# An expert attention's loop, its sections cut anew: next front, own attention, former output in one, and queries and keys loaded in three runs

## The chip, the cores and the metric

The kernel runs on one core of one Trainium2 chip. The metric is the device time of one execution in microseconds, the median of several runs. Besides the runs there is one execution under the hardware profiler, from which all rows come. PE is TensorE, DVE VectorE, ACT ScalarE, POOL GpSimd and SP the queue that issues the direct DMAs.

## The reference

Two transformer layers work on x of 4 x 1024 tokens with 256 channels; every sublayer reads a layer norm of x and is added to it. In the second sublayer of layer 0 each of 4 experts is an attention of its own, with 16 heads of 16 channels, over the tokens whose router picks it:

```python
    for e in range(e_total):
        member = (top2 == e).any(-1)
        ...
        xg = jnp.take_along_axis(x, order[..., None], axis=1)
        ...
        q = (xg @ wq[e] + bq[e]).reshape(b, s, h, hd)
        ...
        att = jnp.einsum('bqhd,bkhd->bhqk', q, k) * sm_scale
        att = jnp.where(validg[:, None, None, :], att, -1000000000.0)
        att = jax.nn.softmax(att, axis=-1)
        y = jnp.einsum('bhqk,bkhd->bqhd', att, v).reshape(b, s, d)
        y = y @ wo[e] + bo[e]
        out = out.at[bidx, order].add(wg[..., None] * y)
```

The first sublayers of both layers are causal attentions over all 1024 tokens of a batch element, the last one is a mixture of 64 expert networks.

## The kernel before

The program has these stages, with a barrier of all engines between them: setup; the first causal attention (`l0`), which also routes tokens and scatters their rows to `xg_d`; the loop over 16 expert units; the second causal attention (`l1`), which gathers the units' outputs from `yg_d`; the expert networks (`last_*`).

A *unit* is one batch element with one expert. Its tokens fill `nt` tiles of 128 rows, 0 to 8; the numbers are known only on the chip, in `cnt`. `unit_loop` (L1496) is a hardware loop in which each engine loads its unit's count and jumps through a tree of choices to a program for that `nt`. Each engine's instructions come from one list of tasks, sorted by nominal times in `unit_order` (L257); every engine walks the list and emits its part (`attention_pe` L381, `attention_act` L530, `attention_dve` L612, `attention_pool` L921, `attention_sp` L998). `Waits` puts a semaphore wait where a task needs another's result.

The tasks of a unit, in the order of its list:

- `mk`, `wo`: SP loads the mask row of the keys and the output weights.
- `xt`: PE transposes the rows in XF (L401), ACT copies them to XT.
- `qp`: four projections, of queries and keys for two halves (`g2`) of the heads (L386). ACT writes the result twice (L567, L568), POOL splits it into three bf16 parts in PH (`spl`, L976 to L980), SP stores PH to `qk_d` (`qs`, L1029) and loads it back into QS or KS with the heads apart and 16 channels on partitions, six blocks of 16 rows (`ql`, L1037).
- `vp`: the values (L417), copied to VA. `bv`, `bb`: the value bias through the output weights (L503).
- `nx` (`next_unit`, L1103): SP loads the next unit's rows into XF and its weights.
- For each of four groups `g` of four heads: `s1`, a first pass of the scores (L430), whose maxima DVE reduces (L627); `mh`, `ml`, `mt`, `mr`: the negated maxima become two rows that SP copies from MR to QS (L1046); then `s2`, the second pass (L448), whose exponentials ACT writes to P (L597), and `pv` (L470), the product with the values. `po` and `nt` turn and normalise the result into ON. The second pass of a group runs beside the first pass of the following one.
- `yt` (L486), `op` (L495, released by DVE L699), `yo` (L1081): transposition, output projection, store to `yg_d`.

The tasks that use the large PSUM tiles share two *slots* in turn; a slot is free again when ACT or DVE has copied or reduced it. At the end SP waits for all its DMAs, then all engines meet in `barrier` (L1477), in which SP clears the semaphores, and jump back. So nothing of one unit runs beside another but the loads of `nx`.

The causal layers use the same tasks, from `causal_order` (L191), with four batch elements running into each other. Their `qs` and `ql` have the forms above with 1024 tokens.

## Time and profile before

| What | Value |
|---|---|
| Median of 3 runs | 5252.07 us (5250.45 to 5259.73) |
| Profiled execution, its own time | 5252.09 us |
| Its span | 5250.3 us |
| PE busy | 3697.0 us, 70% |
| DVE busy | 2276.7 us, 43% |
| ACT busy | 2038.4 us, 39% |
| POOL busy | 1158.3 us, 22% |
| Mean granted TensorE clock | 0.830 |

The span goes from the first to the last instruction. Busy is the time in which an engine had an instruction under way. A clock of 1.0 is 2.4 GHz, 0.5 is 1.2 GHz; a stretch in which both were granted shows a value between. DMA is the mean busy share of 16 DMA engines. In a timeline a row gives start, length, engine, line and operation, and in brackets how long the engine had been idle and what ended that; an fp32 matmul counts as two instructions. The sixteen units stand between 955 and 3592 us, with 6, 2, 3 and 7 tiles, four times over.

### The profile page before, as it was taken

The page shows a single profiled execution, that of the slowest core. Times are in us where ns is not written, and L with a number is a line of the kernel's source. Part 1 is how long each engine was busy: PE and PEld are TensorE (multiplying, and loading weights), DVE is VectorE, ACT ScalarE, POOL GpSimd, SP SyncE. Part 2 cuts the span into 40 slices and gives each one's busy share as a digit, 9 for nine tenths or more (in the row PEclk, how much of TensorE's full clock was granted, in tenths as well). Part 3 has the DMA queues.
Part 4 walks back from the last instruction along what each step waited for, and adds up shares of the span by engine and source line. Part 5 has one row for each costly group of instructions (what it writes and reads, how often), then busy time and mean ns, then how long its engine had stood idle before and what let it go on. Part 6 is the DMA issues. An engine that isn't in the chain of part 4 may idle for free. (4 is left out here: it accounts for less than half of the span.)

```text
span 5250.3 us, 56423 instructions
## 1 busy us (share of the span) xinstructions
PE 3697.0 (70%) x20420; PEld 1654.9 (32%) x20421; DVE 2276.7 (43%) x5427; ACT 2038.4 (39%) x4287; POOL 1158.3 (22%) x969
## 2 busy tenths in 40 slices
PE   3888886575696856968569684694488788816765
PEld 1343443232222322223222232222133333304553
DVE  2656663332363423624136251371566666511222
ACT  1555554252272522726226361262254444500111
POOL 2132233100101011010110101102323463471343
PEclk7999998696797967979679796797699899957887
DMA  4745451503404034040340403402524343002456
GB/s 107 151 124 125 98 147 41 96 16 74 85 1 81 12 79 85 1 81 8 82 84 3 81 7 84 68 18 70 107 66 94 81 89 72 20 19 89 103 132 154
DMA packets 345500, 385.41 MB, mean 73 GB/s; under 512 B 51248, under 2 KB 299056, under 8 KB 344928
## 3 DMA queue, kind: packets, MB, share of 16 engines
q1 hardware_dynamic: 318318, 343.19, 29.8%
q0 software_dynamic: 26624, 35.82, 3.2%
q8 instruction: 224, 3.67, 0.3%
q14 instruction: 334, 2.74, 0.2%
HBM read 224.10 MB, written 145.33 MB: 70 GB/s over the span
## 5 line engine op out<-in xcount | busy, mean ns | idle before, releaser
L597 ACT ACTIVATE P<-PSUM 128x512 f32<-128x512 f32 (+2 forms) x3520 | 1559.7, 501 | 861.4 <-PE PSUM L448 617.4
L448 PE MATMUL PSUM<-QS,KS 101*128 101x512 bf16 (+2 forms) x3520 | 1077.3, 350 | 240.6 <-DMA QS<-MR 138.7
L430 PE MATMUL PSUM<-KS,QS 99*128 99x512 bf16 (+3 forms) x3520 | 1010.2, 376 | 301.2 <-DMA KS<-qk_d 136.3
L627 DVE TENSOR_REDUCE M<-PSUM 128x1 f32<-128x896 f32 (+3 forms) x960 | 942.9, 1024 | 486.5 <-PE PSUM L430 480.4
L470 PE MATMUL PSUM<-P,VA 128*17 128x512 f32 (+3 forms) x7040 | 783.1, 522 | 0.0
L630 DVE TENSOR_REDUCE M<-PSUM 128x1 f32<-128x640 f32 (+6 forms) x704 | 585.5, 832 | 270.8 <-PE PSUM L430 268.6
L976 POOL TENSOR_TENSOR QF<-QF,PH 128x1024 f32<-128x1024 f32 (+4 forms) x96 | 150.0, 1562 | 2462.4 <-ACT PH L568 2455.2
L448 PEld LDWEIGHTS PSUM<-QS,KS 101*128 101x128 bf16 x3520 | 332.3, 100 | 1061.7 <-ACT P L597 644.4
L430 PEld LDWEIGHTS PSUM<-KS,QS 99*128 99x128 bf16 x3520 | 284.2, 103 | 845.4 <-DVE M L627 312.2
L633 DVE CUSTOM_DVE_ANT_0 PSUM<-PSUM,mask 128x128 f32<-128x128 f32 x1024 | 285.1, 301 | 289.6 <-PE PSUM L430 289.6
L401 PE MATMUL PSUM<-ident,XF 128*128 128x128 f32 x272 | 61.4, 390 | 357.2 <-issue 264.0
L984 POOL DMA_INDIRECT list_d<-tlist,dlist x256 | 253.7, 991 | 257.2 <-DVE tokid L919 179.9
L386 PE MATMUL PSUM<-XT,W 128*128 128x512 f32 (+2 forms) x640 | 287.2, 607 | 21.7 <-ACT XT L552 13.3
L589 ACT ACTIVATE MR<-PSUM 8x1024 bf16<-8x1024 f32 (+4 forms) x96 | 73.3, 764 | 466.9 <-PE PSUM L437 466.9
L417 PE MATMUL PSUM<-W,XT 128*128 128x256 f32 x544 | 165.6, 469 | 115.8 <-ACT PH L568 105.7
L451 PE MATMUL PSUM<-maskB,identb 128*128 128x128 bf16 x1024 | 221.7, 231 | 0.0
L685 DVE RECIPROCAL RD<-PSUM 128x16 f32<-128x16 f32 (+2 forms) x160 | 38.1, 238 | 416.1 <-PE PSUM L478 416.1
L470 PEld LDWEIGHTS PSUM<-P,VA 128*17 128x17 f32 x7040 | 139.1, 97 | 233.7 <-issue 205.9
L552 ACT ACTIVATE XT<-PSUM 128x1024 f32<-128x1024 f32 (+2 forms) x40 | 35.3, 894 | 437.7 <-PE PSUM L401 378.9
L567 ACT ACTIVATE QF<-PSUM,bq 128x1024 f32<-128x1024 f32 (+4 forms) x80 | 65.2, 815 | 351.7 <-PE PSUM L386 157.7
L386 PEld LDWEIGHTS PSUM<-XT,W 128*128 128x128 f32 x640 | 137.8, 223 | 154.7 <-issue 99.0
L417 PEld LDWEIGHTS PSUM<-W,XT 128*128 128x128 f32 x544 | 125.9, 238 | 152.9 <-ACT PH L568 117.0
(169 smaller groups left out, 3330.2 us busy)
## 6 DMA issues: line engine op xcount, KB each, us to landing
qk_d<-PH SPq DMA_DIRECT2D x32, 768.0 KB, 3.6
QS<-qk_d SPq DMA_DIRECT2D x96, 256.0 KB, 9.8
KS<-qk_d SPq DMA_DIRECT2D x96, 256.0 KB, 16.7
xg_d<-GX SPq DMA_DIRECT2D x17, 1152.0 KB, 9.7
yg_d<-GX SPq DMA_DIRECT2D x16, 1152.0 KB, 7.6
XF<-xg_d SPq DMA_DIRECT2D x17, 1024.0 KB
VA<-n_L_ffn_expert_gate_up_w SPq DMA_DIRECT2D x64, 256.0 KB, 2.8
qk_d<-PH SPq DMA_DIRECT2D x16, 672.0 KB, 11.3
```

Of the source, the lines that this page charges most:

```text
L386: return e.matmul(out_, W[:, wi, k, cols:cols + 128], XT[:, k, a:a + n], start=(k == 0), stop=(k == 1))
L417: mm = e.matmul(f[:, 256 * x:256 * x + 256], XT[:, k, 128 * t:128 * t + 128], W[:, 2, k, :], start=(k == 0), stop=(k == 1))
L430: mm = e.matmul(slot_heads(s, hb)[:, x, a:b], QS[0:KA, g, h + x, 128 * qt:128 * qt + 128], KS[0:KA, g, h + x, a:b], start=True, stop=True)
L448: mm = e.matmul(SCORE[n % 3][:, 0:q1 - q0], KS[0:KB, g, j, 128 * kt:128 * kt + 128], QS[0:KB, g, j, q0:q1], start=True, stop=not diag, ski ...
L451: mm = e.matmul(SCORE[n % 3][:, 0:128], identb[:, :], maskB[:, :], start=False, stop=True, skip_group_check=True)
L470: mm = e.matmul(PO[32 * j:32 * j + 17, a:b], VA[:, par, kt, 4 * g + j, :], P[:, n % NP, 0:q1 - q0], start=(kt == 0), stop=(kt == kts[-1]), ...
L597: e.activation(P[:, m % NP, 0:q1 - q0], SCORE[m % 3][:, 0:q1 - q0], ACT.Exp, scale=ly.scale).then_inc(S["act_p"], 1)
L627: e.tensor_reduce(m[:, 0, qt, h:h + hb], v[:, :, 0:kn], AX.X, ALU.max).then_inc(S["dve_a"], 1)
L630: e.tensor_reduce(m[:, 0, qt, h:h + hb], v[:, :, 0:kn - 128], AX.X, ALU.max)
L633: mm = e.tensor_tensor_reduce(out=v[:, x, kn - 128:kn], in0=v[:, x, kn - 128:kn], in1=mask[:, :], scale=1.0, scalar=NEG, op0=ALU.add, op1= ...
L976: e.tensor_tensor(f, f, hi, ALU.subtract).then_inc(S["pool_s"], 1)
L984: e.indirect_dma_start(out=list_d, out_offset=bass.IndirectOffsetOnAxis(ap=dlist[:, k:k + 1], axis=0), in_=tlist[:, k // 8:k // 8 + 1], in ...
```

## The change

**Sections.** The loop runs over sections instead of units. Section `u` holds three units under the numbers 0, 1 and 2 of its tasks: the output (`yt`, `op`, `yo`) of unit u - 1, the attention of unit u, and the front (`xt`, `qp`, `spl`, `qs`, and `ql` of the first half) of unit u + 1. `ql` of the second half and its mask stand at the head of the unit's own section. The front is made for 4 tiles where the next count is below 5, and for 8 elsewhere (`Unit(nt, ahead)`), so there are 18 programs instead of 9 (with none for 0 tiles left out), and the engines load two counts. The output is always made for 8 tiles. A `lead` section in front of the loop makes unit 0's front for 8 tiles, a `trail` behind it the last output. The counts of the next unit's rows (XF) are now two units ahead (`nr`), the weights are loaded at a section's head (`nx`), the value weights once the own values are done (`nv`), the output weights once the former output is done (`wo`).

**Loop end.** `barrier` is split: `arrive` at the end of a section, before the jumps, and `meet` in the chosen program, behind the jumps.

**Queries and keys.** `qk_d` has the order part, channel, head, token. `qs` is three DMAs, one for each part; `ql` is three DMAs of 48, 32 and 16 rows instead of six of 16. This holds for `l0` and `l1` too.

**Rows of maxima.** MR has 4, 2 or 1 places, for up to 2, up to 4 and more tiles, and `mt` waits for the row copy that used its place.

Also, `l0` zeroes two more blocks of `xg_d` and one more of `yg_d`, since the block numbers are one higher, and the mask table has 17 rows.

```diff
+class Unit(Layer):
+    def __init__(self, nt, ahead, tail=True):
+        Layer.__init__(self, "moe", 1, nt, False, 0.5)
+        self.tail = tail
+        self.other = {0: Layer("moe", 1, NT, False, 0.5), 2: Layer("moe", 1, ahead, False, 0.5) if ahead else None}
...
 def unit_order(layer):
-    ev = [(t + 1, task) for t, task in attention_steps(layer, 1)]
...
+    nt, ev = layer.nt, []
+    step, alone, rows = 0.84 * nt * nt, 0.6 * nt * nt, 8.0
+    end = 12.0
+    if nt:
+        first = [(0.0, alone / 0.82)] + [(alone + step * g, step) for g in range(3)]
...
+            t = first[g][0] + 0.82 * first[g][1] + rows
...
+        ev += [(-1.0 + 0.1 * w, ("ql", 1, w, 1)) for w in range(2)] + [(-0.7, ("mk", 1, 1))]
+        ev += [(1.0 + 4.0 * c, ("vp", 1, c)) for c in range(layer.nch)]
+        end = second[1][0] + step
+    if layer.tail:
+        for c in range(2):
+            ev += [(2.0 + 4.0 * c, ("yt", 0, c)), (8.0 + 4.0 * c, ("op", 0, c)), (8.5 + 4.0 * c, ("yo", 0, c))]
+    if layer.of(2):
+        ev += [(-0.6, ("nx", 2)), (9.0, ("nv", 2)), (13.0, ("wo", 1)), (19.0, ("bv", 1)), (20.0, ("bb", 1))]
+        x = min(20.0, 9.0 + step)
+        y = 16.0 if step < 20.0 else 25.0
...
+                t = x + 5.0 + y * g2 + 6.0 * w
+                ev += [(t, ("qp", 2, w, g2)), (t + 0.1, ("spl", 2, w, g2)), (t + 6.0, ("qs", 2, w, g2))]
+        ev += [(max(end, x + 21.0) + 0.1 * w, ("ql", 2, w, 0)) for w in range(2)]
...
-                    e.dma_start(qk_d[wi][:, 128 * g2:128 * g2 + 128, 0:n].rearrange("p c n -> c p n"),
-                                PH[:, wi, :, 0:n]).then_inc(S[f"qst{wi}{g2}"], 16)
+                    for p in range(3):
+                        e.dma_start(qk_d[wi][p if wi == 0 else 2 - p, :, 8 * g2:8 * g2 + 8, 0:n].rearrange(
+                            "d h n -> h d n"), PH[:, wi, p, 0:n]).then_inc(S[f"qst{wi}{g2}"], 16)
...
-                    for r, p in enumerate((0, 1, 2, 0, 1, 0) if wi == 0 else (0, 0, 0, 1, 1, 2)):
+                    for r, a, b in ((32, 0, 3), (0, 0, 2), (80, 0, 1)) if wi == 0 else ((32, 0, 3), (0, 1, 3), (80, 2, 3)):
                         e.dma_start(
-                            dst[16 * r:16 * r + 16, 2 * g2:2 * g2 + 2, :, 0:n].rearrange("p g h n -> p (g h) n"),
-                            qk_d[wi][p, 128 * g2:128 * g2 + 128, 0:n].rearrange("(h d) n -> d h n", d=16)).then_inc(
+                            dst[r:r + 16 * (b - a), 2 * g2:2 * g2 + 2, :, 0:n].rearrange("p g h n -> p (g h) n"),
+                            qk_d[wi][a:b, :, 8 * g2:8 * g2 + 8, 0:n].rearrange("m d h n -> (m d) h n")).then_inc(
                             S[f"qld{wi}{g2}"], 16)
...
+                def program(nt, ahead):
+                    meet(e, key)
+                    section(units[nt, ahead], v)
+                    arrive(e, key)
...
-                    elif lo > 0:
-                        unit(lo, v)
...
+                        with e.If(after < 5):
+                            program(lo, 4)
+                        with e.Else():
+                            program(lo, NT)
...
-                barrier(e, key)
+            meet(e, key)
```

PE, before: end of the program for 2 tiles and start of the one for 3. L486 and L495 are the output, L401 to L503 the front, L430 the first pass of the scores, L437 the maxima, L448 the second pass. A number behind x counts equal instructions in a row.

```order
L486 MATMUL PSUM<-ident,ON 128x128 x4
L495 MATMUL PSUM<-W,YT 128x256 x4
L1507 UNCONDITIONAL_BRANCH
L1505 COMPARE_AND_BRANCH
L401 MATMUL PSUM<-ident,XF 128x128 x6
L386 MATMUL PSUM<-XT,W 128x384 x8
L417 MATMUL PSUM<-W,XT 128x256 x6
L503 MATMUL PSUM<-W,BVB 128x256 x2
L430 MATMUL PSUM<-KS,QS 128x384 x12
L437 MATMUL PSUM<-identb,MHL 8x128 x3
L430 MATMUL PSUM<-KS,QS 128x384 x2
L448 MATMUL PSUM<-QS,KS 128x384 x2
```

PE, with the change: start of the section for 3 tiles (behind the jump). L483 is the first pass, L470 the values, L539 and L548 the former unit's output, L490 the maxima.

```order
L1592 COMPARE_AND_BRANCH
L483 MATMUL PSUM<-KS,QS 128x384 x4
L470 MATMUL PSUM<-W,XT 128x256 x6
L483 MATMUL PSUM<-KS,QS 128x384 x2
L539 MATMUL PSUM<-ident,ON 128x128 x8
L483 MATMUL PSUM<-KS,QS 128x384 x8
L490 MATMUL PSUM<-identb,MHL 8x128 x3
L539 MATMUL PSUM<-ident,ON 128x128 x8
L483 MATMUL PSUM<-KS,QS 128x384 x4
L548 MATMUL PSUM<-W,YT 128x256 x8
L483 MATMUL PSUM<-KS,QS 128x384 x6
L490 MATMUL PSUM<-identb,MHL 8x128 x3
```

Before, the front stood ahead of all scores and the output behind them, each in one piece; now the first pass is first, and values and the former output stand between pieces of it.

SP, before: program for 3 tiles, from the first store of queries to the load of the next rows.

```order
L1029 DMA qk_d<-PH 128x3x384
L1037 DMA QS<-qk_d 16x8x384 x6
L1029 DMA qk_d<-PH 128x3x384
L1037 DMA KS<-qk_d 16x8x384 x6
L1029 DMA qk_d<-PH 128x3x384
L1037 DMA QS<-qk_d 16x8x384 x6
L1029 DMA qk_d<-PH 128x3x384
L1037 DMA KS<-qk_d 16x8x384 x6
L1106 ISA
L1106 DMA XF<-xg_d 128x8x256
```

SP, with the change: end of the section for 3 tiles that prepares 8. L1169 loads XF, L1103 copies rows of maxima, L1085 stores, L1094 loads, L1128 loads the mask.

```order
L1169 DMA XF<-xg_d 128x8x256
L1103 DMA QS<-MR 1x4x384 x2
L1085 DMA qk_d<-PH 8x16x1024 x6
L1094 DMA QS<-qk_d 48x8192
L1094 DMA QS<-qk_d 32x8192
L1094 DMA QS<-qk_d 16x8192
L1094 DMA KS<-qk_d 48x8192
L1094 DMA KS<-qk_d 32x8192
L1094 DMA KS<-qk_d 16x8192
L1128 ISA
L1128 DMA KS<-mk_d 1x8x1024
L1085 DMA qk_d<-PH 8x16x1024 x6
```

Before, stores and loads of the own unit alternated ahead of the scores; now two stores' worth of six DMAs come before the loads of the first half and two behind them, at the section's end, in shapes of 8 x 16 and of 48, 32 and 16 rows.

## Rows read from the trace of the kernel before

**Rows 1.** The page: span of the profiled execution.
```profile
span 5250.3 us, 56423 instructions
```

**Rows 2.** Windows of units 4 to 7: stretch, length, busy per engine, clock, DMA, GB/s.
```profile
1616.70:1655.80 39.10, 24.43 (x73) 16.65 (x74) 0.71 (x2) 9.79 (x12) 16.35 (x12) 0.81 0.63 105
1655.80:1809.30 153.50, 133.67 (x814) 42.38 (x814) 92.36 (x118) 88.11 (x203) 0.00 (x0) 0.88 0.19 33
1809.30:1831.00 21.70, 7.23 (x40) 5.98 (x39) 2.42 (x4) 1.90 (x3) 0.00 (x0) 0.79 0.14 44
1831.00:1849.80 18.80, 11.84 (x32) 8.40 (x33) 0.72 (x2) 4.44 (x10) 6.88 (x12) 0.68 0.33 96
1849.80:1893.00 43.20, 25.93 (x142) 11.60 (x142) 12.38 (x22) 12.68 (x39) 0.00 (x0) 0.50 0.23 66
1893.00:1908.30 15.30, 5.38 (x14) 3.52 (x14) 1.19 (x3) 0.98 (x2) 0.00 (x0) 0.61 0.06 20
1908.30:1934.40 26.10, 14.50 (x38) 8.64 (x38) 0.75 (x2) 5.72 (x10) 9.26 (x12) 0.70 0.49 96
1934.40:1991.50 57.10, 36.60 (x213) 12.76 (x213) 24.99 (x38) 23.85 (x55) 0.00 (x0) 0.79 0.24 59
1991.50:2017.00 25.50, 6.02 (x23) 4.31 (x22) 1.55 (x3) 1.30 (x2) 0.00 (x0) 0.65 0.08 22
2017.00:2061.00 44.00, 26.48 (x79) 17.37 (x80) 0.72 (x2) 11.18 (x12) 18.72 (x12) 0.81 0.69 118
2061.00:2252.70 191.70, 172.50 (x949) 49.64 (x949) 122.25 (x134) 114.44 (x235) 0.00 (x0) 0.89 0.17 29
2252.70:2282.00 29.30, 8.49 (x45) 7.06 (x45) 2.77 (x4) 2.21 (x3) 0.00 (x0) 0.72 0.19 54
```

**Rows 3.** Windows of the first stage: 7, 2 and 3 tiles.
```profile
2061.00:2096.50 35.50, 27.45 (x65) 4.48 (x65) 30.74 (x31) 0.91 (x1) 0.00 (x0) 0.50 0.90 152
1849.80:1866.00 16.20, 3.24 (x15) 1.61 (x16) 3.92 (x5) 0.37 (x1) 0.00 (x0) 0.50 0.60 174
1934.40:1953.70 19.30, 5.95 (x17) 1.30 (x17) 6.77 (x9) 0.48 (x1) 0.00 (x0) 0.50 0.70 173
```

**Rows 4.** Timeline between units 7 and 8: last DVE operation, first matmul.
```profile
2262.28 0.96 DVE L699 TENSOR_TENSOR XR<-PSUM,BOB 128x768 f32<-128x768 f32 x1 [1.36 <-PE PSUM L495]
...
2282.03 2.82 PE L401 MATMUL PSUM<-ident,XF 128*128 128x128 f32 x12 [19.79 <-issue]
```

**Rows 5.** Timeline of the first layer around two projections.
```profile
368.41 0.42 DVE L630 TENSOR_REDUCE M<-PSUM 128x2 f32<-128x256 f32 x1 [3.09 <-PE PSUM L430]
...
370.45 0.50 PE L430 MATMUL PSUM<-KS,QS 99*128 99x384 bf16 x2 [1.79 <-ACT PH L568]
...
376.49 4.35 PE L386 MATMUL PSUM<-XT,W 128*128 128x512 f32 x8
```

**Rows 6.** Timeline: values (first layer), then transpositions and output projection of unit 7.
```profile
54.69 5.77 PE L417 MATMUL PSUM<-W,XT 128*128 128x256 f32 x26
...
2253.78 1.82 PE L486 MATMUL PSUM<-ident,ON 128*128 128x128 f32 x14
...
2255.93 6.31 PE L495 MATMUL PSUM<-W,YT 128*128 128x256 f32 x28 [0.33 <-ACT YT L552]
```

**Rows 7.** Timeline of POOL in the first layer: a split of 8 tiles.
```profile
57.77 2.13 POOL L976 TENSOR_TENSOR QF<-QF,PH 128x1024 f32<-128x1024 f32 x1
...
59.96 1.04 POOL L978 CAST PH<-QF 128x1024 bf16<-128x1024 f32 x1
...
61.07 2.12 POOL L980 TENSOR_TENSOR PH<-QF,PH 128x1024 bf16<-128x1024 f32 x1
```

**Rows 8.** DMA from 58 to 93 us (40 slices), and the timeline at its end.
```profile
DMA  1991000999999999999999999999999999999999
GB/s 54 391 384 70 0 0 12 374 272 187 302 112 129 133 112 150 110 140 115 122 138 117 143 110 138 122 129 129 115 143 110 143 117 124 138 110 146 103 121 298
...
92.89 0.58 PE L430 MATMUL PSUM<-KS,QS 99*128 99x128 bf16 x4 [32.42 <-DMA KS<-qk_d]
```

**Rows 9.** Timeline: first transposition of unit 0; load of x in the last attention.
```profile
955.07 2.82 PE L401 MATMUL PSUM<-ident,XF 128*128 128x128 f32 x12 [53.49 <-issue]
...
3608.84 0.94 SPq L1009 DMA_DIRECT2D XF<-x_d  x2
```

More of the change, by code:

```diff
@@ L124, in at, with earlier @@
         return self.value[name, task]
+    def earlier(self, task):
+        return self.layer.name == "moe" and task not in self.present
     def evacuated(self, task):
@@ L142, in wait_ge @@
     def wait_ge(self, name, *task):
-        if len(task) > 1 and isinstance(task[1], int) and task[1] < 0:
+        if task[1] < 0 or self.order.earlier(task):
             return
@@ L1116, in build @@
         l0 = causal_order(Layer("l0", B, NT, True, 0.25))
         l1 = causal_order(Layer("l1", B, NT, True, 0.25))
-        units = {nt: unit_order(Layer("moe", 1, nt, False, 0.5)) for nt in range(1, NT + 1)}
+        units = {(nt, a): unit_order(Unit(nt, a)) for nt in range(NT + 1) for a in (4, NT)}
+        lead, trail = unit_order(Unit(0, NT, False)), unit_order(Unit(0, None))
         def setup_sp(e):
@@ L1568, in _ @@
             barrier(e, "dve")
-            unit_loop(e, "dve", lambda nt, v: attention_dve(e, units[nt], units[nt].layer))
+            attention_dve(e, lead)
+            unit_loop(e, "dve", lambda O, v: attention_dve(e, O))
+            attention_dve(e, trail)
             barrier(e, "dve")
-            attention_dve(e, l1, l1.layer)
+            attention_dve(e, l1)
             barrier(e, "dve")
```

303 lines of the change are left out of this document (170 added, 133 removed).

## The prediction

> **What bounds the kernel now.** I read the views in the order of the row groups. The page gives the span [rows 1]. The windows of four neighbouring units [rows 2] show the loop as it repeats: units of 6, 2, 3 and 7 tiles take 214.3, 77.3, 108.6 and 265.0 us, together 665.3, four times over. Each unit stands there in three rows. The first is its front, from the first transposition to the first score matmul: 39.1 + 18.8 + 26.1 + 44.0 = 128.0. The second is its attention: 153.5 + 43.2 + 57.1 + 191.7 = 445.5. The third is output, barrier and the way into the next program: 21.7 + 15.3 + 25.5 + 29.3 = 91.8.
>
> In the 6-tile front PE is busy 24.4 of 39.1 us, DVE 0.7: it is a chain of projection, split on POOL, store and load. In attention PE is busy 87 to 90% for 6 and 7 tiles, but 60 and 64% for 2 and 3. [Rows 3] show the first stage, when only group 0's scores run. With 7 tiles DVE is busy 30.7 of 35.5 us and PE has half its clock (0.50); with 2 and 3 tiles 16.2 and 19.3 us pass with PE busy 3.2 and 6.0, since the second pass waits for the row DMA. After a unit's last DVE operation PE starts nothing for 19.8 us [rows 4]. So 220 of 665 us are front and end. The question is what that work costs once it stands beside attention.
>
> **What moves, and its price.** A projection of 8 tiles in the first layer's stream of scores holds PE 4.35 us. DVE stood idle 3.09 before its next reduce, and PE then waited 1.79 for the two ACT copies that free the slot [rows 5]: 3.1 + 1.8, about 5 us; for 4 tiles about half, 2.7. The values take 5.77 us for 26 half-instructions, so 3.6 for 4 tiles or 0.95 a tile; the output projection 6.31 for 28, so 3.6 for 4 tiles, and 4.5 with its release on DVE; its transpositions 1.82 for 14, so 2.1 for 4 tiles [rows 6]. I take 2.5 for a chunk of XT and 1.5 for the bias product, estimates from the same rows.
>
> Front and output no longer follow the unit's own length: the output is always 8 tiles, a front 4 or 8. The sections are 6 (ahead 4), 2 (ahead 4), 3 (ahead 8) and 7 (ahead 8). Output and bias cost 2 x (2.1 + 4.5) + 1.5 = 14.7 in each. With values, XT and four projections the added work is for 6: 5.7 + 14.7 + 2.5 + 10.8 = 33.7; for 2: 1.9 + 14.7 + 2.5 + 10.8 = 29.9; for 3: 2.9 + 14.7 + 5.0 + 20.0 = 42.6; for 7: 6.7 + 14.7 + 5.0 + 20.0 = 46.4. Together 152.6.
>
> What covers them: with 6 and 7 tiles, seven pieces stand in the DVE-bound first stage, where each overlaps one reduce of about 1 us (7), and the row trip at its end is filled (5). With 2 and 3 tiles the waiting of [rows 3] takes up 12 each; MR's slots, which end a group's wait for the former row, are in that figure. In the 2-tile unit PE is at half clock throughout its attention [rows 2]; kept busy it should rise, 8 us off. This cover is 4 x 12 + 8 = 56.
>
> What is late next: a section waits for all its DMAs. In the 2- and 3-tile sections the last projection of the next front stands at the end, behind the scores. After it come ACT's copies, a split, 2.13 for the subtraction, 1.04 for the cast and as much as the first again for the second subtraction, 5.3 us at 8 tiles [rows 7], and a store; SP has the loads of group half 0 queued ahead of that store. I add 8 us (2 tiles) and 10 (3 tiles), between nothing and case A below. With 6 and 7 tiles attention outlasts this chain by far.
>
> The end: the output's store is gone from it, and PE jumps ahead on its own while SP still waits. One more level of choice is added, with a taken jump where the next unit needs 8. I take 12, 8, 10 and 15 us, between 7 (the gap behind the 2-tile unit less its store) and the 19.8 of [rows 4].
>
> Sections: 6: 153.5 + 33.7 - 12 + 12 = 187.2 (214.3 now); 2: 43.2 + 29.9 - 12 - 8 + 8 + 8 = 69.1 (77.3); 3: 57.1 + 42.6 - 12 + 10 + 10 = 107.7 (108.6); 7: 191.7 + 46.4 - 12 + 15 = 241.1 (265.0). Together 605.1 for 665.3: 60.2 less, four times: **-241**.
>
> **Lead and trail.** Unit 0's front now runs alone, with 8 tiles: weights about 7 us (they are loaded behind the barrier now), first projection and copies 6, then splits that wait in turn for a store and the copies, the last done near 40, its store 8 more: 48 us. The loop's jumps come behind it, 8. It begins some 13 us ahead of today's first transposition at 955.07 [rows 9], whose jumps come first. Net +43. The trail does unit 15's output alone on a cold PE, 18 us, and the load of w1_o and its landing come after it. L1's other loads, which today stand alone between barrier and barrier, go beside it. Net +18.
>
> **The loads.** At the first layer's start the 16 DMA engines are 90% busy or more. Stores of queries move 374 to 391 GB/s, loads mostly 110 to 143, and PE starts at 92.89 after 32.42 us of waiting [rows 8]. A store reads 128 partitions, a load writes 16. The new loads write 48, 32 and 16, on average twice as wide; I take twice the rate, between no gain and the store's rate. Inside the loop no front waits for a load any more, so it pays at the start of the two causal layers: 8 us each, **-16** (0 to -24). The Trainium skill (SBUF — State Buffer, Door 1: the DMA port swizzle) says that DMA bandwidth depends on how many of 16 ports the partitions reach; by its map 16 neighbours reach 4, rows 0 to 31 reach 8 and rows 32 to 79 reach 12. By it the two wider loads reach two and three times the ports; the trace agrees in the rates above.
>
> At nothing I cost two more zeroed blocks (beside the first layer's 950 us), the wider semaphore clear and the second count read. If their cover failed they would show as a few us.
>
> **Sum.** -241 + 43 + 18 - 16 = -196. The profiled execution took 5252.09 us for a span of 5250.3; the median of the runs is 5252.07, so nothing has to be converted. Forecast: **5056 us**.
>
> **Rivals.** A. *Small sections last as long as the chain of the next front.* Their attention is 43 and 57 us; the chain has four splits, four stores and two loads, and the section's end waits for all. For it: in today's 2-tile unit this chain takes 18.8 us [rows 2] for 2 tiles, and now 4 or 8 are prepared. The store changes too: three DMAs whose far side has 8 heads outermost instead of 128 rows. If a store took 2 us more and the loads queued ahead of the last one, sections 2 and 3 would be 16 us longer and the lead 8: 4 x 32 + 8 = 136, 5192. Against it: the order places two of the four projections well before the end. The Trainium skill (DMA: Bandwidth & Descriptors, Why a DMA increments its semaphore by 16 and not by 1) has a rule for the store: the engines used are the largest number up to 16 that divides the slowest dimension of both sides; that is 8 here, half of them. By it this part of case A happens; I can read no such transfer in the trace of before.
>
> B. *The pieces cost PE's time alone, and no chain sticks out.* By the rows' PE times they are 28.5 + 24.9 + 36.5 + 40.1 = 130, 23 less than charged, and the 18 for the chains fall away: 4 x 41 = 164, 4892. Against it: PE is already 90% busy in the 7-tile attention [rows 2].
>
> C. *Slower: PE keeps half its clock.* [Rows 3] show 0.50 in the first stage with PE busy 77%, and each section begins behind 8 us or more of idle. If all the added 130 us per four sections ran at 1.2 instead of 2.4 GHz, that would add 4 x 130 = 520. The kernel is slower than before from 196 / 520 = 38% of it on; at 60% it is 5368. Against it: in the 6- and 7-tile fronts, with the same projections, 0.81 was granted [rows 2].
>
> D. *No cover.* The slots hold two tasks only; if no piece ran beside a reduce or a row trip, 4 x 56 = 224 would come back: 5280. Against it: the 12 us in the small units are idle of every engine.
>
> **Numbers.** Forecast 0.59, A 0.19, B 0.13, C 0.06, D 0.03. Around the forecast, cover (12 per four sections), ends (4 each) and loads leave 5000 to 5115. The range takes in A and most of the way to B: 4940 to 5195. A measurement of this kernel can tell from no change what is over 0.2%, 10.5 us. C and D fall on the slow side or near none: faster 0.91, same 0.02, slower 0.07.
>
> **What would show it.** Four sections, from one 6-tile section's first score matmul to the next one's, near 605 us, single ones near 187, 69, 108 and 241. Clock near 1.0 in a 7-tile section's first 35 us; 0.5 means C. DVE idle some 3 us before each projection's end. In the 2- and 3-tile sections PE idle at the end while SP waits for a store or load: over 15 us means A. The first layer's first score matmul near 85, and loads there above 200 GB/s. The forecast is wrong in kind if four sections take over 650 us.

## The result and the profile after

| | median us | lowest to highest | runs |
|---|---|---|---|
| before | 5254.94 | 5250.45 to 5259.73 | 4 |
| changed | 5321.34 | 5319.14 to 5329.98 | 4 |

The ratio is 1.0129, with an interval of 1.0112 to 1.0147: **66 us slower**, where the forecast was 5056 us, 196 faster, in a range of 4940 to 5195. The profiled execution has a span of 5317.4 us, against 5250.3 [rows 1]. Later runs were made on other chips too, on some of which both kernels took 2.4% longer (the kernel before 5375 to 5380 us), and by the trace of e3, below, all of that lies ahead of the units and behind them (31 and 100 us). So versions are compared by their ratio to the kernel before on the same chip, and inside the trace by the length of a batch of four units.

The head of the page of the changed kernel:

```profile
span 5317.4 us, 57933 instructions
## 1 busy us (share of the span) xinstructions
PE 3751.1 (71%) x20880; PEld 1723.0 (32%) x20881; DVE 2299.0 (43%) x5440; ACT 2067.5 (39%) x4306; POOL 1229.6 (23%) x981
```

Where the time is: the windows of the changed kernel's second batch, the same units as in [rows 2]. Each section has two rows, from its first score matmul to PE's last matmul (I call it PE's part), and from there to the next section's first score matmul (the end). The columns are those of [rows 2].

```profile
1673.60:1859.80 186.20, 162.37 (x916) 63.98 (x916) 95.45 (x122) 95.82 (x217) 11.70 (x12) 0.91 0.21 49
1859.80:1875.00 15.20, 0.00 (x0) 0.00 (x0) 0.50 (x2) 0.00 (x0) 0.00 (x0) 0.56 0.05 10
1875.00:1928.70 53.70, 42.25 (x228) 25.55 (x228) 15.95 (x28) 19.75 (x50) 6.15 (x7) 0.90 0.30 85
1928.70:1959.90 31.20, 0.01 (x1) 0.02 (x2) 0.00 (x0) 1.27 (x2) 5.53 (x6) 0.57 0.44 97
1959.90:2052.20 92.30, 73.57 (x328) 36.03 (x328) 28.92 (x42) 36.76 (x69) 16.82 (x10) 0.87 0.42 97
2052.20:2089.20 37.00, 0.05 (x2) 0.03 (x2) 0.59 (x2) 0.00 (x0) 4.34 (x3) 0.51 0.24 64
2089.20:2325.30 236.10, 203.23 (x1080) 75.26 (x1080) 126.07 (x138) 128.23 (x250) 21.17 (x12) 0.93 0.23 54
2325.30:2345.20 19.90, 0.03 (x2) 0.02 (x2) 0.59 (x2) 0.00 (x0) 0.00 (x0) 0.60 0.06 12
sum 671.60, PE 481.51 PEld 200.89 DVE 268.07 ACT 281.82 POOL 65.72; mean PE 60.19 PEld 25.11 DVE 33.51 ACT 35.23 POOL 8.21
```

Four sections take 671.6 us where four units took 665.3 and 605.1 were forecast. (This batch is a long one: the mean of three is 666.3, against 664.5 before.) Split by what PE does, the two batches read like this:

| us of a batch | before [rows 2] | changed | difference |
|---|---|---|---|
| PE busy | 473.1 | 481.5 | +8.4 |
| PE idle in fronts of their own | 50.8 | 0 | -50.8 |
| PE idle in the attention part | 76.8 | 86.8 | +10.0 |
| PE idle in output and end; now in the ends | 64.7 | 103.3 | +38.6 |
| sum | 665.3 | 671.6 | +6.3 |

The fronts' idle 50.8 us did go. Of that, 38.6 came back between the sections, 10.0 inside them, and 8.4 as more work of PE, at a clock that is higher than before in most stretches: a front is now made for 4 or 8 tiles, the output always for 8.

By measured stretches of the whole span, the +67.1 us are: +58.0 from 955.1 (unit 0's first transposition, [rows 9]) to 1013.1 (the first section's first score matmul), which is the lead; +17.3 over sections 1 to 15; -16.8 over the last one with the trail, up to the first transposition of `l1`; +8.6 in all that follows. What was forecast for the 16 sections, -241, is missing almost whole.

What an end consists of, first the one behind the 3-tile section. This is the chain of waits of the changed kernel from 2045 to 2090 us: start, length, engine or queue, operation. "PEldq" and "SPq" are the sequencers of PE and SP; L1085 is the store of the front's queries and keys, L1574 the head of the loop, L1576 and L1577 the loads of the two tile counts, L1587 and L1592 the tree that leads to the program of a section, L1554 the meeting of the engines. "issue" is time in which the queue waited for nothing that the profile shows.

```profile
2051.26 2.13 POOL QF L1031
...
2053.44 1.04 POOL PH L1033
...
2054.52 2.17 POOLq L1546
2056.71 0.56 SPq L1085
...
2057.32 0.80 SPq L1085
...
2058.16 10.93 DMA qk_d<-PH
...
2069.60 4.27 issue
2073.87 0.04 SPq L1574
...
2074.03 5.45 issue
...
2081.05 0.04 SPq L1587
2081.09 2.37 issue
2083.47 0.04 SPq L1587
2083.51 3.00 issue
...
2086.61 0.04 SPq L1592
2086.65 2.04 issue
2088.69 0.11 SPq L1554
```

Everything stands in a row. The last split on POOL, the last store, 10.9 us until it has landed, and only then does SP begin to jump: to the loop's head, to the counts, through the tree. 19.6 us pass from the landing at 2069.1 to the meeting at 2088.7, 17.1 of them in five pieces of 2.0 to 5.5 us, each behind a jump, in which SP waits for nothing that the profile shows. PE's own jumps, begun at 2052.4, are over at 2079.2.

The other kind of end stands behind the 7-tile section, the same chain from 2324 to 2346 us:

```profile
2324.16 0.50 ACT OT L660
...
2325.46 3.87 PEldq L1594
...
2329.49 4.81 PEldq L1574
...
2335.89 3.71 PEldq L1587
2339.60 0.06 issue
2339.66 0.07 PEldq L1587
2339.73 0.06 issue
2339.79 4.96 PEldq L1587
...
2345.18 0.84 PE PSUM L483 x2
```

Here SP has been done for long, and PE's own jumps fill it: 3.87 out of the tree, 4.81 to the loop's head, 3.71 and 4.96 into the tree are 17.4 of the 19.9 us. A branch that is not taken (L1587 at 2339.66) costs 0.07. Not every taken jump is long: behind the 2-tile sections PE's way out of the tree and back to the loop's head took 0.18 and 0.23. In the kernel before, the barrier stood between a unit's end and the loop's jump, and output work of other engines ran over the exit from the tree; PE's long jumps between unit 7 and unit 8, inside the 19.79 us of [rows 4], are three, not four.

### The profile page after: what moved, and what is told of

Read it like the earlier page. It is cut to its first block, busy times and chain, and to the rows that moved or that the text cites. A ratio compares the mean times of both kernels' runs of the same rounds, so it can differ in the third digit from the quotient of the medians.

```text
span 5317.4 us, 57933 instructions
## 1 busy us (share of the span) xinstructions
PE 3751.1 (71%) x20880; PEld 1723.0 (32%) x20881; DVE 2299.0 (43%) x5440; ACT 2067.5 (39%) x4306; POOL 1229.6 (23%) x981
## 4 chain that ended last, share of the span: by engine, by line
PE 44%; DVE 20%; issue 9%; POOL 8%; ACT 8%; DMA 7%; PEldq 2%; SPq 1%; POOLq 0%; ACTq 0%; PEld 0%; DVEq 0%; another core or an unknown queue 0%
PE PSUM L523 10%; DVE M L682 8%; PE PSUM L501 7%; PE PSUM L483 6%; DVE M L685 5%; PE PSUM L436 5%; PE PSUM L548 4%; POOL list_d L1039 3%; PE PSUM L470 3%; ACT P L651 2%; DMA qk_d<-PH 2%; DVE PSUM L688 2%; PE PSUM L1365 2%; DMA ye_d<-P,lists 1%; DMA P<-xw_d,lists 1%
## 5 line engine op out<-in xcount | busy, mean ns | idle before, releaser
L483 PE MATMUL PSUM<-KS,QS 99*128 99x512 bf16 (+3 forms) x3520 | 934.5, 354 | 735.0 <-SPq L1560 422.8
L501 PE MATMUL PSUM<-QS,KS 101*128 101x512 bf16 (+2 forms) x3520 | 1052.7, 344 | 140.0 <-ACT P L651 126.1
L1031 POOL TENSOR_TENSOR QF<-QF,PH 128x1024 f32<-128x1024 f32 (+1 forms) x100 | 177.9, 1779 | 2518.6 <-ACT PH L622 2511.4
L483 PEld LDWEIGHTS PSUM<-KS,QS 99*128 99x128 bf16 x3520 | 283.1, 101 | 1184.0 <-SPq L1560 429.5
L436 PE MATMUL PSUM<-XT,W 128*128 128x512 f32 x656 | 343.4, 669 | 19.4 <-DVE M L682 7.6
L633 ACT ACTIVATE VA<-PSUM 128x1024 f32<-128x1024 f32 (+2 forms) x40 | 35.7, 896 | 578.6 <-PE PSUM L470 578.6
L548 PE MATMUL PSUM<-W,YT 128*128 128x256 f32 x800 | 214.0, 428 | 6.0 <-DVE M L682 2.8
L621 ACT ACTIVATE QF<-PSUM,bq 128x1024 f32<-128x1024 f32 (+1 forms) x84 | 78.2, 931 | 324.7 <-PE PSUM L436 291.9
L548 PEld LDWEIGHTS PSUM<-W,YT 128*128 128x128 f32 x800 | 170.2, 218 | 45.8 <-DVE M L682 9.7
L1035 POOL TENSOR_TENSOR PH<-QF,PH 128x1024 bf16<-128x1024 f32 (+1 forms) x100 | 178.0, 1780 | 8.0
L470 PE MATMUL PSUM<-W,XT 128*128 128x256 f32 x544 | 162.4, 463 | 18.8 <-DVE M L682 9.7
## 6 DMA issues: line engine op xcount, KB each, us to landing
xg_d<-GX SPq DMA_DIRECT2D x19, 1152.0 KB, 10.9
```

Source lines behind the costliest of these rows:

```text
L436: return e.matmul(out_, W[:, wi, k, cols:cols + 128], XT[:, k, a:a + n], start=(k == 0), stop=(k == 1))
L470: mm = e.matmul(f[:, 256 * x:256 * x + 256], XT[:, k, 128 * t:128 * t + 128], W[:, 2, k, :], start=(k == 0), stop=(k == 1))
L483: mm = e.matmul(slot_heads(s, hb)[:, x, a:b], QS[0:KA, g, h + x, 128 * qt:128 * qt + 128], KS[0:KA, g, h + x, a:b], start=True, stop=True)
L501: mm = e.matmul(SCORE[n % 3][:, 0:q1 - q0], KS[0:KB, g, j, 128 * kt:128 * kt + 128], QS[0:KB, g, j, q0:q1], start=True, stop=not diag, ski ...
L548: mm = e.matmul(f[:, 256 * x:256 * x + 256], YT[:, k, 128 * t:128 * t + 128], W[:, 3, k, :], start=(k == 0), stop=(k == 1))
```

## The experiments

Theories: **1**, the small sections end in a serial tail in which SP waits for the last store and then jumps; **2**, pieces of front and output cost what PE and ACT work on them, wherever they stand; **3**, the new form of the stores, with 8 heads outermost, is slow; later **4**, the jumps of PE and SP bound every end; and **5**, in the first stage the pieces hold a PSUM slot that the scores for DVE's reduces need. The column "batch" is read from PE's rows: the distance from the start of the first 7-tile section to that of the fourth (in the kernels without sections, of the 7-tile unit's front), over three.

| kernel | edit | ratio to before | interval | batch, us |
|---|---|---|---|---|
| before | | 1 | | 664.5 |
| changed | | 1.0129 | 1.0112 to 1.0147 | 666.3 |
| e0 | the changed kernel on another chip | 1.0137 | 1.0117 to 1.0157 | 666.7 |
| e1 | late waits | 1.0043 | 1.0028 to 1.0058 | 658.9 |
| e2 | old DMA forms, sections kept | 1.0146 | 1.0123 to 1.0169 | 664.0 |
| e3 | before, new DMA forms alone | 0.9953 | 0.9937 to 0.9970 | 658.4 |
| e4 | early front | 1.0049 | 1.0032 to 1.0065 | 656.7 |
| e5 | e1 and e4 | 1.0008 | 0.9991 to 1.0026 | 652.3 |
| e6 | no output in the sections | 0.9750 | 0.9730 to 0.9769 | 616.2 |
| e7 | no front in the sections | 0.9483 | 0.9451 to 0.9515 | 573.6 |
| e9 | e5 and loop hint | 0.9934 | 0.9918 to 0.9951 | 641.5 |
| e11 | e5 and pieces behind the first stage | 0.9964 | 0.9945 to 0.9983 | 644.3 |
| e12 | e9 and e11 | 0.9884 | 0.9863 to 0.9905 | 634.3 |
| e13 | before, new DMA forms, loop hint | 0.9866 | 0.9842 to 0.9890 | 644.3 |
| e14 | e9 without the choice by the next unit | 1.0162 | 1.0135 to 1.0188 | 674.4 |

e8 and e10 put a jump table in place of the tree, on e5 and on the kernel before. They gave no result, so what a table costs stays open.

### The changed kernel again

> The changed kernel as it is, beside the others on one chip, since the chip of the first four runs took 2.4% longer for the kernel before than the chip of the first comparison. All theories: ratio 1.011 to 1.015 to the kernel before.

1.0137. It holds on another chip, and ratios of the two comparisons may be set side by side.

### e1, late waits

```diff
             for name in DMA_SEMS:
-                w.wait_all(name)
+                if not (moe and O.layer.of(2) and name in LATE):
+                    w.wait_all(name)
...
-        def meet(e, key):
+        def meet(e, key, units=False):
             if key == "sp":
+                if units:
+                    for name in LATE:
+                        e.wait_ge(S[name], 48)
```

LATE holds the four stores' and the two loads' semaphores of the next unit's front.

> Edit: in a section the sync engine (SP) no longer waits at its end for the four stores and the two loads of the next unit's front; it waits for them after its own jumps, just before the semaphores are cleared. Theory 1 (the small sections end in a serial tail: store lands, then SP's jumps of 11.8 and 18.2 us start): the 6.9 and 9.5 us for which SP waited before its jumps, after the sections of 2 and 3 tiles of batch 1, lie under the jumps, 16 us a batch, 60 to 70 us in all, about 5255. Theory 2 (the loss is what the added pieces take of PE and ACT within the sections): no more than 10 us. Theory 3 (the new form of the stores is slow): the stores end late in any case, the gain is as in theory 1 at most half.

1.0043 against 1.0137 is some 50 us, near the 60 to 70 of theory 1 and well above theory 2's 10. A batch gives 7.8 us and the lead another 5 to 7 (63.6 us in e0 and 65.5 in the first profile to 58.2, from its first transposition to the first score matmul). That is 36 to 39 us; for the rest no single stretch stands out.

The gain is half of the 16 us a batch that was expected, since SP's wait was not alone. Behind the 3-tile sections the end falls from 35 to 29 us on average, and now PE's own jumps, which start with its last matmul and take 21 to 27 us, end 4 to 6 us before the next section starts.

### e2 and e3, the DMA forms

e2 puts one store of all three terms and six loads of 16 rows back into the changed kernel; e3 puts the three stores and three loads into the kernel before:

```diff
-                    e.dma_start(qk_d[wi][:, 128 * g2:128 * g2 + 128, 0:n].rearrange("p c n -> c p n"),
-                                PH[:, wi, :, 0:n]).then_inc(S[f"qst{wi}{g2}"], 16)
+                    for p in range(3):
+                        e.dma_start(qk_d[wi][p if wi == 0 else 2 - p, :, 8 * g2:8 * g2 + 8, 0:n].rearrange(
+                            "d h n -> h d n"), PH[:, wi, p, 0:n]).then_inc(S[f"qst{wi}{g2}"], 16)
...
-                    for r, p in enumerate((0, 1, 2, 0, 1, 0) if wi == 0 else (0, 0, 0, 1, 1, 2)):
+                    for r, a, b in ((32, 0, 3), (0, 0, 2), (80, 0, 1)) if wi == 0 else ((32, 0, 3), (0, 1, 3), (80, 2, 3)):
```

> Edit: the sections of the changed kernel stay, the stores and loads of queries and keys get the forms of before (one store of three terms, six loads of 16 rows, the old layout in DRAM). Theories 1 and 2: within 15 us of the changed kernel, 5306 to 5336, since a store landed in about 9 to 10 us in either form. Theory 3 (the stores whose outer dimension is 8 heads hold the section ends and the first layer back): 60 us or more faster, under 5260.

> Edit: the kernel before with the new forms of stores and loads and nothing else. My prediction's term for the loads: 16 us faster than before, about 5239. From the trace after (first layer's first score 2.2 us earlier, its end 2.6 us later): 0 to 5 us slower, 5255 to 5260. Theory 3: 60 us or more slower than before.

e2: 1.0146, no different from the changed kernel. Theory 3 falls, and with it most of the DMA half of my rival A: by the batches (664.0 for 666.7 in e0) the new forms cost the sections some 3 us at most, most of it at the ends behind 3 tiles (33 us on average for 35). The lead is no shorter with the old form (65.5 us, against 65.5 and 63.6). e3: 0.9953, **25 us faster** than before, more than the 16 that I had booked and against my reading after the result (0 to 5 slower). But most of it does not lie where I put it: a batch is 6.1 us shorter, and from unit 0's first transposition to that of `l1` the kernel is 22 us shorter. The starts of the two causal layers give less than the 8 us each that I booked. In the changed kernel the first layer's first score matmul came at 90.7 instead of 92.9 [rows 8], where I expected 85; in `l1` it came 69.9 us behind the first transposition instead of 75.2. e3 shows the same (90.0 and 70.8), and e2, with the old forms, gives both back (95.1 and 74.2). Between sections, where loads run beside attention, the same forms bring nothing (e2).

### e4 and e5, the front earlier in the small sections

```diff
         y = 16.0 if step < 20.0 else 25.0
+        if nt <= 3:
+            x, y = 3.0, (11.0 if nt <= 2 else 14.0)
```

> Edit: in sections of 0 to 3 tiles the next unit's front is placed at 3.0 instead of 11.3 to 16.6 in the planner's time, and its second halves 11 or 14 behind the first. Theory 1: the last store of the 2-tile and 3-tile section starts 8 to 15 us earlier, the idle ends after them (31.2 and 37.0 us) fall to 20 to 25, the sections take 0 to 5 us more inside: 15 to 25 us a batch, 60 to 100 in all, about 5240. Theory 2 (pieces cost the same wherever they stand): within 20 us of 5321. Slower than 5321 if the early transposes and projections stand before the reduces' scores in PE's queue and delay the first stage by more than the ends give.

> Both edits: SP waits for the stores and loads of the front after its jumps, and the front stands at 3.0 in sections of 0 to 3 tiles. Theory 1: the gains add (46 and 42 us by the ratios of the first call against 1.0129), 80 to 90 us under the changed kernel, ratio to before 0.995 to 0.998. If both cure the same wait, only 50 to 60 us, ratio 1.002 to 1.003. Theory 2: no more than either alone.

e4: 1.0049, some 47 us against e0. The end of the 2-tile section falls from 31 to 25 us, that of the 3-tile section from 33 to 37 down to 28 to 32, and PE's parts stay near (52 and 89 to 95 us for 54 and 90 to 92). So the same pieces cost less at another place: theory 2 alone does not explain the ends. e5: 1.0008, 69 us under e0, between "they add" and "they cure the same wait". The gains overlap: in e5 the 2-tile end is 22.5, the 3-tile end 26 to 29 us, although in the latter the last store was issued 7 us before PE's last matmul. That led to theory 4.

One wait was overlooked. The front's mask load (`mk`, KS<-mk_d) is not in LATE. In e5 SP still waits for it behind the 3-tile section, some 12.8 us, and starts its jumps only when it has landed, 6 us behind PE's last matmul. SP's last jump then ends within 5 us of PE's. The kernels that build on e5 keep this wait (11 to 14 us), and no run has it in LATE. PE's own jumps end 0.2 to 6 us before the next start there, and in e12 4 to 7.5; so the wait can be worth some 6 us at each of four ends, and no more.

### e6 and e7, the pieces left out

```diff
+    if layer.tail and nt:
+        ev = [(t, task) for t, task in ev if task[0] not in ("yt", "op", "yo")]
```

e7 leaves out the next unit's "xt", "qp", "spl", "qs" and the load "nr" in the same way.

> Leaves out, in the 16 sections, the output of the former unit: the transposes of its heads, the output projection with its bias and the store; the output of every unit but the last is missing. Theory 1 (pieces are partly covered): 5 to 7 us less a section, 80 to 110 us less in all. Theory 2 (no cover): 10 to 14 us a section, 160 to 220 us less.

> Leaves out, in the 16 sections, the next unit's transposes of the input, its projections of queries and keys, their splits and their stores, and the load of the rows; loads of queries and keys, value projections and attention stay, so every unit works on what the lead left. In the kernel before this work took 128 us a batch as stages of its own, loads and values included. Theory 1: 20 us less in the sections of 6 and 7 tiles, 30 to 45 in those of 2 and 3, of which half at the section ends: 110 to 130 us a batch, 440 to 520 in all. Theory 2 (only what PE and ACT work on it counts, and that is half covered): 60 to 80 a batch, 240 to 320 in all.

e6 is 0.9750 against 1.0137: 208 us, 13 a section, in theory 2's span and twice theory 1's. PE's parts of its second batch:

```profile
1660.90:1834.10 173.20, 153.30 (x868) 54.26 (x868) 93.07 (x120) 93.74 (x215) 11.69 (x12) 0.89 0.21 46
1849.00:1893.00 44.00, 33.46 (x180) 17.36 (x180) 13.40 (x26) 17.65 (x48) 6.11 (x7) 0.81 0.28 79
1922.00:1998.10 76.10, 61.43 (x280) 24.95 (x280) 26.59 (x40) 34.71 (x67) 16.84 (x10) 0.86 0.45 106
2029.50:2254.20 224.70, 194.64 (x1032) 66.19 (x1032) 123.75 (x136) 126.07 (x248) 21.15 (x12) 0.92 0.22 52
```

They are 13.0, 9.7, 16.2 and 11.4 us shorter than with the output (in the changed kernel's second batch), 50.3 together, of which PE's own busy time is 9.1 + 8.8 + 12.1 + 8.6 = 38.6. I had priced the same pieces (without the bias product, which stays) at 13.2 each, 52.8, and then taken 12 off every section as covered. **For the output there is no cover in the large sections**: it costs PE's own time there and 3 to 4 us more, though DVE is idle for about half of such a section (95.5 of 186.2 us busy).

e7 is 0.9483: 351 us, 22 a section, between the two spans. PE's parts fall by 15 to 24 us in all but the 2-tile section (9), and the 2-tile end halves, 31 to 16. But the end of the 3-tile section, without any store or split, is still 24 to 28 us, and that of the 7-tile section does not move (19.4). These two are not the front's chain: behind 7 tiles PE's own jumps end 0.2 to 0.3 us before the next section starts, behind the first three 3-tile sections 0.3 to 1.1.

### e9, the loop hint

```diff
-            with e.Fori(0, B * E0) as u:
+            with nc.Fori(0, B * E0, engines=bass.OrderedEngineSet([e.engine]), hint_back_edge=True) as u:
```

Each engine is told at the top of the body where its closing branch will lead.

> Edit on top of e5_late_early: each engine is told of the loop's closing branch at the top of the body (a prefetch hint), nothing else. Theory 4: the jump back (4 to 6 us on PE, 5 us on SP) and perhaps the count load's fetch behind it fall out of every section end, 4 to 8 us a section, 60 to 120 us in all, ratio 0.978 to 0.990. If the hint is lost on the way (other branches within the body) or the jumps do not count: ratio 0.998 to 1.003.

0.9934 against 1.0008 is 39 us, where I expected 60 to 120: the effect is there, smaller than its price in the rows. The same end as above, behind the 7-tile section, in the chain of waits of e9 (L1583 is the loop's head now, L1596 the tree):

```profile
2274.77 3.42 PEldq L1603
...
2278.42 2.90 PEldq L1583
...
2283.02 3.52 PEldq L1596
...
2286.74 4.69 PEldq L1596
```

The jump to the loop's head is 2.90 instead of 4.81, not nothing; the end is 17.2 instead of 19.9. The ends behind 6 and 3 tiles fall by about 2 us too, and the one behind the 2-tile section, which waits for SP, from 22.2 to 23.2 in e5 to 17.5 to 18.3: a batch gives 10.8 us in all.

### e11, the pieces out of the first stage

In sections of 5 tiles and more, output and front stand behind the first stage:

```diff
+            o = alone + 4.0 if nt >= 5 else 0.0
+            ev += [(o + 2.0 + 4.0 * c, ("yt", 0, c)), (o + 8.0 + 4.0 * c, ("op", 0, c)),
...
+        if nt >= 5:
+            x = late + 16.0
```

> Edit on top of e5_late_early: in sections of 5 to 8 tiles the output of the former unit and the front of the next one stand behind the first stage (score tiles of group 0 reduced on DVE) instead of in it. Theory 5 (in the first stage the pieces hold one of the two PSUM slots that the reduces' scores need, so that DVE idles 1 to 4.5 us at each): the sections of 6 and 7 tiles lose their 12 us per output to 6 to 8 each, 4 to 7 us a section of these 8, 30 to 55 us in all, ratio 0.991 to 0.996. Theory 2 (a piece costs the same wherever it stands): 0.999 to 1.002. Slower if the second stage, whose PE is busy 131 of 148 us, takes them in full and gives nothing back in the first.

0.9964, with an interval (0.9945 to 0.9983) that lies below e5's (0.9991 to 1.0026): some 23 us, 8 us a batch. The large sections' parts are 231.6 and 181.5 for 232.5 to 237.5 and 183.9 to 186.6 in e5:

```profile
2037.30:2268.90 231.60, 204.41 (x1080) 72.84 (x1080) 126.22 (x138) 127.92 (x250) 21.22 (x12) 0.92 0.23 55
2288.50:2470.00 181.50, 160.62 (x916) 62.63 (x916) 95.58 (x122) 96.38 (x217) 11.71 (x12) 0.90 0.21 50
```

On average the 6-tile section gives 5.6 us and the 7-tile one 2.7, where 4 to 7 were expected of each. PE's idle time falls by 2.5 and 6.0 us; its busy time falls by 3 in the one and rises by 3 in the other. Theory 5 holds for 3 to 6 of the 12 us, and theory 2 for the rest. That it is the slot, and not another wait of the first stage, is argued and not shown.

The first stage of the changed kernel's 7-tile section shows where the time stood. Up to the first matmul of the second pass:

```profile
2089.20:2161.80 72.60, 53.57 (x190) 28.15 (x190) 38.83 (x40) 11.08 (x11) 8.33 (x5) 0.83 0.40 95
```

It takes 72.6 us, where before it took 35.5 with DVE busy 30.7 and PE 27.5 [rows 3]. So 37.1 of the 44.4 us by which this section grew are its first stage. PE is busy 74% of it and DVE 53%: the stage is no longer bound by DVE, and no engine is busy throughout. In e11 it takes 47.4 to 48.1 us, in the 6-tile sections 39.7 to 42.9 where it was 57 to 59; most of what is saved there is spent again behind it.

### e14, one level of jumps less

```diff
-                        with e.If(after < 5):
-                            program(lo, 4)
-                        with e.Else():
-                            program(lo, NT)
+                        program(lo, NT)
```

> Edit on e9_loop_hint (0.9934): no choice by the next unit's tiles, every section carries a front of 8 tiles, so one level of jumps is gone and the units before those of 2 and 3 tiles carry 4 tiles of front more. Theory 4 (each jump of PE at an end costs its 5 us): the end of the 3-tile section falls from 24 to 26 us to 19 to 21, that of the 2-tile section by 2 to 5; against that 5 to 9 us more in each of the sections of 6 and 2 tiles, ratio 0.995 to 1.000 in all. If the ends stay as they are, the jump did not bound them.

Both halves of the reason show, and my size for one was far off: 1.0162, where 0.995 to 1.000 was expected. The window rows of e14, part and end of the sections of 6, 2 and 3 tiles:

```profile
1710.70:1911.10 200.40, 172.58 (x940) 69.81 (x940) 95.43 (x122) 100.19 (x218) 21.16 (x12) 0.90 0.26 61
1911.10:1924.10 13.00, 0.03 (x1) 0.00 (x0) 0.50 (x2) 0.00 (x0) 0.00 (x0) 0.64 0.03 9
1924.10:1990.20 66.10, 53.58 (x252) 30.63 (x252) 16.56 (x28) 23.21 (x51) 15.88 (x9) 0.86 0.48 122
1990.20:2013.50 23.30, 0.02 (x1) 0.03 (x2) 0.00 (x0) 2.12 (x2) 5.27 (x3) 0.57 0.38 105
2013.50:2108.00 94.50, 74.08 (x328) 35.67 (x328) 32.36 (x42) 36.55 (x69) 21.16 (x12) 0.85 0.42 105
2108.00:2127.20 19.20, 0.04 (x1) 0.00 (x0) 0.59 (x2) 0.00 (x0) 0.00 (x0) 0.53 0.20 63
```

The 3-tile section, whose work is the same as in e9, ends in 19.2 to 22.6 us (mean 20.9 of the first three; the fourth leads to another program) instead of 24.3 to 26.6 (25.2): one jump less is worth 4.3 us, about its length on PE (4.65 to 4.89 at the last level in e9). So a jump at such an end counts nearly in full, as theory 4 says; with it gone, PE is through 2.0 to 3.7 us before the next start, and SP is last. Against it, four more tiles in the fronts ahead of the 2- and 3-tile units cost 13 to 17 us in the 6-tile section (mean 14) and 16 to 21 (mean 19) with the end in the 2-tile one, for 10 to 11 of PE's busy time each on average. Padding a front by four tiles costs three to four times what a level of choice does.

### e12 and e13, the best of each

> All four edits on the changed kernel: late waits of SP, early front in sections of 0 to 3 tiles, loop hint, pieces behind the first stage in sections of 5 to 8 tiles. Theory 4 and 5 (different waits): the gains of e9_loop_hint (39 us against e5) and e11_pieces_stage2 (23 us) add: ratio 0.987 to 0.991 to the kernel before. If they cure the same wait: 0.992 to 0.994.

> The kernel before with the new forms of the stores and loads (0.9953 alone) and the loop hint, without the sections. Its loop jump stands in the ends after the sections of 7 and 6 tiles only (3.3 to 4.1 us on PE; after 3 tiles 0.2): 0 to 3 us at each of 8 ends, ratio 0.991 to 0.995. If it comes out at or below e12_combined, the sections bring nothing over fronts of their own.

e12: 0.9884 (0.9863 to 0.9905), where 0.987 to 0.991 meant that the waits are different ones. It beats the kernel before by 1.2% and the changed one by 2.5%. The ends of e12 behind 6, 2, 3 and 7 tiles, and the sum of all eight windows:

```profile
1852.80:1865.90 13.10, 0.04 (x1) 0.04 (x2) 0.50 (x2) 0.00 (x0) 0.00 (x0) 0.60 0.04 9
...
1918.40:1936.70 18.30, 0.02 (x1) 0.03 (x2) 0.00 (x0) 1.27 (x2) 2.92 (x3) 0.55 0.17 50
...
2028.40:2054.70 26.30, 0.05 (x1) 0.05 (x2) 0.59 (x2) 0.00 (x0) 0.00 (x0) 0.52 0.22 57
...
2287.80:2304.90 17.10, 0.02 (x1) 0.03 (x2) 0.59 (x2) 0.00 (x0) 0.00 (x0) 0.54 0.05 12
sum 632.30, PE 477.98 PEld 195.38 DVE 271.86 ACT 282.15 POOL 65.77; mean PE 59.75 PEld 24.42 DVE 33.98 ACT 35.27 POOL 8.22
```

632.3 us: the ends are 74.8 instead of 103.3, PE's idle time inside the sections 79.7 instead of 86.8.

e13, the old structure with two small edits, comes out at 0.9866 (0.9842 to 0.9890), better than expected (0.991 to 0.995) and no different from e12. Its batch is 10 us longer than e12's, four times 40 us, and it has no lead, which cost 58 us in the changed kernel and 5 to 7 less with the late waits. **The sections, at their best as tried here, bring nothing over fronts of their own.** Up to some 22 us may be left in e12, by the mask wait of e5; that was not tested. Of the two edits e13 and e9 share, the stores and loads are worth 25 us in the kernel before (e3), and the hint 47 more. The traces of e3 and e13 show where: PE's idle time ahead of a unit's first transposition falls from 15, 8, 17 and 19 us (behind 6, 2, 3 and 7 tiles) to 11.5, 6, 13.4 and 17, 11 us a batch. PE's jumps of over 1 us sum to 131 us in e3 (34 of them) and to 87 in e13 (23): the loop's own jump went from 3.3 to 4.0 down to 0.4 to 0.5, and four of those in the tree are gone too. I had looked at the loop's jump alone, behind 6 and 7 tiles.

## Why the prediction was wrong, by its own steps

**Sections, -241 forecast.** By the second batch, PE's part and end against the forecast (its ends are the "12, 8, 10 and 15" and its late chains the "8" and "10"):

| section | PE's part forecast | measured | end forecast | measured |
|---|---|---|---|---|
| 6 tiles | 175.2 | 186.2 | 12 | 15.2 |
| 2 tiles | 53.1 | 53.7 | 8 + 8 | 31.2 |
| 3 tiles | 87.7 | 92.3 | 10 + 10 | 37.0 |
| 7 tiles | 226.1 | 236.1 | 15 | 19.9 |
| sum | 542.1 | 568.3 | 63 | 103.3 |

- **The ends are the step that failed most**, 40 of the 66 us of a batch. "After it come ACT's copies, a split ... and a store" was the right chain, and "PE jumps ahead on its own while SP still waits" was true of PE. What I did not put in the row is SP's own way: it jumps only after the landing, 19.6 us behind the 3-tile section and 12 behind the 2-tile one. And I took PE's jumps from [rows 4] as a ceiling, "19.8 us", when one more level (4.3 us, e14) and the exit from the tree were added to an end that has no output work left to hide them. Rival A, at 0.19, named the small sections and gave them 16 us each, near the 15 and 17 us that their ends were over the forecast. But its cause was the front's chain with a slower store. By e2 the store's form hardly matters, and by e1, e5 and e14 the jumps behind the chain are as large a part as the chain.
- **The cover failed next.** "What covers them: ... seven pieces stand in the DVE-bound first stage". The 6-tile section took 33.7 us of added work and grew by 32.7, the 7-tile one 46.4 and grew by 44.4: cover 1.0 and 2.0 instead of 12 each. 3 tiles: 7.4 of 12. 2 tiles: 19.4 of 20, the one place where it held, with the clock at 0.90 for 0.50 as forecast. Prices of the pieces were right in the main (50.3 against 52.8 us for the output, e6; 20.7 to 24.4 against 25.0 for a front of 8 tiles with 3 and 7, and 15.0 and 8.6 against 13.3 for one of 4 tiles with 6 and 2, e7). In the first stage the pieces delayed DVE instead of running beside it: that stage of the 7-tile section is 37.1 us longer, and by e11 3 to 6 us of the 12 come back once they stand elsewhere. Rival D, "no cover", was given 0.03; for the large sections it is what happened.
- The first stage's clock did rise, to 0.83 from 0.50 with 7 tiles. Rival C did not come true. The reason that I gave against B ("PE is already 90% busy") speaks against any cover as well.

**Lead and trail.** +43 forecast, +58 measured. The splits were done 41 us behind the lead's first transposition where I had 33, the last store took 17.5 us from its first issue to its landing (14.2 from its last one) where I had 8, and the way through SP's jumps then 7. For the trail, last section and way into `l1` together I had -6 and got -17.

**Loads, -16 forecast at l0 and l1.** At the starts of the two layers the changed kernel gained 2.2 and 5.3 us where I had 8 each. What follows the start of `l1` is 13.9 us longer, which is open. In the kernel before, the same forms give 25 us (e3), but mostly in the units, 6.1 us a batch, and the sections hide that (e2).

**Sum.** Forecast and measured span differ by 263 us (-196 against +67). Over sections 1 to 15, all batches and not only the second, the ends hold 144 us of it and the missing cover 84. The lead with the first layer holds 23, what follows from `l1` on 17, and the last section with the trail takes 11 back. Some 6 are left, since the four units of [rows 2] were longer than the others. The text's own alarm, "wrong in kind if four sections take over 650 us", went off at 671.6.

The Trainium skill (Runtime: NRT & Kernel Launch, Instruction fetch mechanics) says that instructions are fetched ahead in sequence only, and that a taken branch to code outside the window held by the engine stalls until that code is fetched. I had not set it against this change, which adds programs (9 to 18), a level of choice, and ends with nothing to hide the way through them. The trace agrees in the main: in the changed kernel PE's long jumps last 3.3 to 7.8 us each and those not taken 0.07 to 0.08, while the taken ones out of the 2-tile sections and back to the loop's head last 0.2. No trace here shows the fetch itself.

Open: why a hint for the loop's jump shortens jumps in the tree as well; what the new forms shorten in e3 (of the 6 us of a batch 2 lie in the fronts and 5 in the attention, and the ends are 1 longer); why the changed kernel is 9 us longer from `l1` on. A jump table in place of the tree, which would test theory 4 more directly, has no result.

## What to carry to other kernels

Before work is moved into a busier stretch, look at the engine that will carry it: here PE was busy 87 to 90% of the large attentions, and the work added to it cost its full time and about a third more (50.3 us for 38.6 of PE, e6), though DVE and ACT were idle for about half of the time. When stages are merged, list what stood over the jumps and waits at their border, since it no longer does; let each engine jump first and wait for its transfers behind the jumps, and place the last chain of stores so that it is issued before the busiest engine ends. Test the small parts of a change alone on the old kernel: here two of them (new loads, a loop hint) reach what the whole restructuring reaches at its best.

## What the runs showed of the hardware

- In the changed kernel 54 of PE's jumps last 3.3 to 7.8 us each, in their own rows; on SP the row is 0.04 us and the cost stands behind it as 1.9 to 5.5 us of "issue". Five such in a row behind the 3-tile section are 25 us of PE. The taken ones out of the 2-tile section and from there to the loop's head cost 0.2. The page's busy times hold none of it.
- Telling the engines of the loop's closing branch mostly shortened PE's jump there (4.6 to 7.1 us in e5; 2.9 to 3.6 in e9, but 6.5 and 5.9 behind two of the 3-tile sections), and the kernel by 0.7%. In the kernel before it shortened it from 3.3 to 4.0 us (e3) to 0.4 to 0.5 (e13).
- The last store of a front, 256 KB in each of three DMAs, landed 10.9 us after its last issue behind the 3-tile section and 14.2 in the lead. As one DMA (e2) it took 9.2 and 21.6.
- PE's granted clock in the sections of 2 tiles was 0.90 where the same attention alone had 0.50 [rows 2], the lower of its two levels (1.2 of 2.4 GHz); the 10.5 us by which that section grew for 29.9 us of added work, as priced, include this.
